# Grouped-query attention: the output projection in rounded parts, and its slots moved

## The chip, the cores and the metric

The kernel runs on one core of one Trainium2 chip. The metric is the device time of one execution in microseconds (us); the lower, the better. The page of the profile and the trace come from one profiled execution.

## What is computed

The program is eight layers on one stream x of 1024 tokens by 256, each of them `x = x + layer(layernorm(x))`: masked attention, a mixture of experts, a gated convolution, the mixture again, a selective scan, a second mixture, grouped-query attention, and the second mixture again. The change lies in the grouped-query attention alone. Cut to what matters:

```python
q = rms_norm(x @ Wq, q_norm_w)          # 32 heads of 128
k = rms_norm(x @ Wk, k_norm_w)          # 4 heads of 128
v = x @ Wv
q, k = rope(q), rope(k)
attn = softmax(causal(q @ k.T / sqrt(128)))
return (attn @ v) @ Wo                  # Wo: 4096 x 256
```

## The kernel before, in words

`gqa_layer` writes out the program of each engine by hand; engines meet only at semaphores. The 32 heads are 8 quads of four, which share one key head; 1024 tokens are 8 blocks of 128. One query tile is a quad's four heads for one block, so there are 64 tiles. Two tiles, a narrow one (block t) and a wide one (block 7 - t), make a **band** with 9 blocks of keys between them; t is 0, 1, 2, 3 in turn, so the wide tile has 1024, 896, 768 or 640 columns of scores. There are 32 bands, counted from 0, and each has 9 **slots**, 0 to 8. In slots 0 to 7 TensorE does one score job each (even slots the narrow tile, odd slots the wide one, one head a job), and in every slot it transposes and weighs one cell (one block of keys of the band before). Other work has its slot by a table: a tile's queries are projected in slots 0 and 6 (`query_tile`, "project"), transposed in slots 2 and 4 ("turn"), and the output projection of a tile, in two halves of two heads each, stands in slots 1, 3, 5 and 7 (`out_pair`).

Per slot and engine, in the order of the queue:

- TensorE: the score (L1333, its mask last, L1335), the transposes of a cell's probabilities (L1343), the query projection (L1268) or the transposes of queries (L1278), the output projection (L1366), and the weighing of the cell before (L1354).
- VectorE: the row maximum (L1226), the first add of the slot before's projection into the stream (L1219), the low part of the cell (L1231), the second add, then rope (L1149 to L1151) of the slot before's query projection or the low part of queries (L1156). Adds thus come one slot after their projection.
- ACT: the copy of a finished tile's output out of PSUM (L1106), the high part of the cell (L1112), the exponentials (L1121), the sums of squares of queries (L1056) or their high part (L1063).
- POOL: the scale of each query tile and the sum and product that end its rope (L1019 to L1027).

Queries are projected into, and transposed into, one PSUM bank (`q_bank`). So `turn_queries(n)` of slot 2 waits until the rope of the tile that slot 0 projected has read the bank, and `project(n)` until the queries before are read:

```python
pe.wait_ge(q_ready, n + 1)
if n % 2:
    pe.wait_ge(q_low_ready, n)
else:
    pe.wait_ge(roped, n + 2)
```

Most operands are split beforehand into a rounded high part and a low part (`F32R`), and `three` gives three matmuls of such parts for one product. The output projection is the exception: it multiplies `oT` and `wo` in plain fp32, two matmuls a half. The output weights of two quads lie in `wo` side by side, and query weights in `w_q` are replaced by SP once their split is done. In the profile's names `gqa_ln_xn` holds the queries after rope, `acc` and `aux` are PSUM, and `stream` is x.

Of the kernel before, what the change touches and what calls it, by code (L numbers as in the profile page):

```python
# [11 lines left out]
F32 = mybir.dt.float32  # L12
F32R = mybir.dt.float32r
# [3 lines left out]
ALU = mybir.AluOpType  # L17
# [3 lines left out]
P = 128  # L21
# [776 lines left out]
def gqa_layer(nc, core, wq_dram, wkv_dram, wo_dram, norm_w_dram, cos_dram, sin_dram):  # L798
# [5 lines left out]
    with ExitStack() as ctx:  # L804
# [4 lines left out]
        norm = Norm(nc, core, ctx, sem, "gqa", whole=False)  # L809
        RING = 4  # L810
        w_q = sb("w_q", [P, DC * QUAD * HD])
        w_q_high = sb("w_q_high", [P, DC * QUAD * HD], F32R)
        w_q_low = sb("w_q_low", [P, DC * QUAD * HD], F32R)
        wo = sb("wo", [P, 2, QUAD, D])
        norm_w = sb("norm_w", [P, 2, HD])
# [25 lines left out]
        sin_k = early[:, 8192:9216].rearrange("p (t d) -> p t d", d=HD)  # L841
        w_kv_high, w_kv_low = probsT_high, probsT_low
        straight = norm.xn[:, 0:4, :].rearrange("p (r a) d -> p r (a d)", r=2)
# [9 lines left out]
        w_q_in = sem("w_q_in")  # L853
        wo_in = [sem("wo_in0"), sem("wo_in1")]
        made = sem("made")
# [43 lines left out]
        TILES = 2 * BANDS  # L899
        SLOTS = CELLS * (BANDS + 1) + 5  # L900

# [37 lines left out]
        def out_pair(z):  # L939

            band, c = divmod(z, CELLS)
            n, half = {1: (2 * band - 3, 0), 3: (2 * band - 3, 1), 5: (2 * band - 2, 0), 7: (2 * band - 2, 1)}.get(c, (-1, 0))
            return (n, half) if 0 <= n < TILES else None
# [5 lines left out]
        def new_quad(z, at):  # L949

            band, c = divmod(z, CELLS)
            return band // 4 + 1 if c == at and band % 4 == 2 and band // 4 + 1 < QUADS else None

        block = ctx.enter_context(nc.Block())

        @block.sync
        def _(sp):
            def load_q(quad):
                sp.dma_start(w_q[:, :], wq_dram[quad:quad + 1].rearrange("a p k n -> (a p) (k n)")).then_inc(w_q_in, 16)

            def load_wo(quad):
                sp.dma_start(wo[:, quad % 2, :, :], wo_dram[quad:quad + 1].rearrange("a h p n -> p (a h) n")).then_inc(wo_in[quad % 2], 16)

            sp.dma_start(w_kv, wkv_dram.rearrange("g p k n -> p g (k n)")).then_inc(w_kv_in, 16)
            load_q(0)
            sp.dma_start(norm_w[:, :, :].rearrange("p a d -> p (a d)"),
                         norm_w_dram.rearrange("(b a) d -> b (a d)", b=1).to_broadcast([P, 2 * HD])).then_inc(norm_w_in, 16)
            sp.dma_start(core.xnT[:, 0, :], cos_dram.rearrange("p t d -> p (t d)")).then_inc(tables_in, 16)
            sp.dma_start(core.xnT[:, 1, :], sin_dram.rearrange("p t d -> p (t d)")).then_inc(tables_in, 16)
            load_wo(0)  # L970
            load_wo(1)
            for quad in range(1, QUADS):
                sp.wait_ge(w_q_low_ready, quad)
                load_q(quad)
                if quad >= 2:
                    sp.wait_ge(wo_done, 2 * NT * (quad - 1))
                    load_wo(quad)

        @block.gpsimd
        def _(pool):  # L980
# [54 lines left out]
            keys(3)  # L1035
            for n in range(3, TILES):
                queries(n)

        @block.scalar
        def _(act):  # L1040
            norm.scalar(act)

            def split_q(quad):
                act.wait_ge(w_q_in, 16 * quad + 16)
                if quad >= 1:
                    act.wait_ge(projected, NT * quad)
                act.activation(w_q_high[:, :], w_q[:, :], ACT.Copy).then_inc(w_q_high_ready, 1)

# [36 lines left out]
            for g in range(KV):  # L1085
                act.activation(w_kv_high[:, g, :], w_kv[:, g, :], ACT.Copy).then_inc(w_kv_high_ready, 1)
            split_q(0)
# [13 lines left out]
            for z in range(SLOTS):  # L1101
                for n in ended(z):
                    act.wait_ge(weighed, last_cell(n) + 1)
                    if n >= 2:
                        act.wait_ge(wo_done, 2 * (n - 1))
                    act.activation(oT[:, n % 2, :], out_bank, ACT.Copy).then_inc(oT_copied, 1)  # L1106
# [23 lines left out]
                if quad is not None:  # L1130
                    split_q(quad)

        @block.vector
        def _(dve):
            norm.vector(dve)

            def split_q(quad):
                dve.wait_ge(w_q_high_ready, quad + 1)
                dve.tensor_tensor(w_q_low[:, :], w_q[:, :], w_q_high[:, :].bitcast(F32), ALU.subtract).then_inc(w_q_low_ready, 1)

# [42 lines left out]
            for g in range(KV):  # L1183
                dve.wait_ge(w_kv_high_ready, g + 1)
                dve.tensor_tensor(w_kv_low[:, g, :], w_kv[:, g, :], w_kv_high[:, g, :].bitcast(F32), ALU.subtract).then_inc(w_kv_low_ready, 1)
            split_q(0)
# [35 lines left out]
            for z in range(SLOTS + 1):  # L1222
# [25 lines left out]
                if quad is not None:  # L1248
                    split_q(quad)

        @block.tensor
        def _(pe):
# [1210 lines left out]
```

## Time and profile before

| what | value |
|---|---|
| median of the runs shown | 1947.77 us (1946.73 to 1949.39, 3 runs) |
| the profiled execution | 1948.34 us |
| its span | 1946.4 us |
| busy: TensorE, VectorE, ACT, POOL | 80%, 65%, 48%, 34% of the span |
| granted TensorE clock, mean over the span | 0.888 |

The profiled execution is 1.9 us longer than its span and 0.6 us over the median. The grouped-query attention takes the span's part from some 930 us to 1800 us. The shares above are means over all layers; what a change in this layer is worth is read from this layer's stretch. PEclk is the TensorE clock that was granted, 1.00 for 2.4 GHz and 0.50 for 1.2 GHz. A matmul's shown end is modelled and overlaps the next one's start, so the time of one matmul in a row of them is read from start to start. In a timeline row the first number is the start in the span, the second the length, and the bracket the idle time of the engine ahead of it with what ended it.

### The profile page before, as it was taken

The page shows a single profiled execution, that of the slowest core. Times are in us where ns is not written, and L with a number is a line of the kernel's source. Part 1 is how long each engine was busy: PE and PEld are TensorE (multiplying, and loading weights), DVE is VectorE, ACT ScalarE, POOL GpSimd, SP SyncE. Part 2 cuts the span into 40 slices and gives each one's busy share as a digit, 9 for nine tenths or more (in the row PEclk, how much of TensorE's full clock was granted, in tenths as well). Part 3 has the DMA queues.
Part 4 walks back from the last instruction along what each step waited for, and adds up shares of the span by engine and source line. Part 5 has one row for each costly group of instructions (what it writes and reads, how often), then busy time and mean ns, then how long its engine had stood idle before and what let it go on. Part 6 is the DMA issues. An engine that isn't in the chain of part 4 may idle for free. (4 is left out here: it accounts for less than half of the span.)

```text
span 1946.4 us, 28135 instructions
## 1 busy us (share of the span) xinstructions
PE 1556.5 (80%) x9150; PEld 1214.7 (62%) x9158; DVE 1264.2 (65%) x2128; ACT 931.6 (48%) x2281; POOL 658.9 (34%) x671
## 2 busy tenths in 40 slices
PE   6899789779864565382769999999999999998373
PEld 4444578668851222272648888888888888886262
DVE  4665354665466998544737777777777777775533
ACT  2365344234424331252536666666666666664341
POOL 3011260415057674704832222222222222220703
PEclk9899799888987888586879999999999999999586
DMA  3321333213420000444000000000000000000443
GB/s 75 53 50 45 115 101 125 76 50 112 127 61 0 0 1 21 153 142 135 25 0 12 1 23 1 23 1 23 1 23 1 23 1 12 1 1 1 163 142 103
DMA packets 75322, 98.28 MB, mean 50 GB/s; under 512 B 11168, under 2 KB 58912, under 8 KB 75184
## 3 DMA queue, kind: packets, MB, share of 16 engines
q1 hardware_dynamic: 69040, 79.71, 13.9%
q0 software_dynamic: 6144, 16.79, 2.7%
q8 instruction: 79, 1.29, 0.3%
q14 instruction: 59, 0.48, 0.1%
HBM read 62.38 MB, written 27.66 MB: 46 GB/s over the span
## 5 line engine op out<-in xcount | busy, mean ns | idle before, releaser
L1226 DVE TENSOR_REDUCE gqa_neg_max<-acc 128x1 f32<-128x1024 f32 (+7 forms) x256 | 192.9, 754 | 175.6 <-PE acc L1335 174.4
L1112 ACT ACTIVATE gqa_probsT_high<-aux 128x512 fp32r<-128x512 f32 x288 | 172.0, 597 | 249.9 <-PE aux L1343 249.1
L1231 DVE TENSOR_TENSOR gqa_probsT_low<-aux,gqa_probsT_high 128x512 fp32r<-128x512 f32 x288 | 197.6, 686 | 29.8 <-ACT gqa_probsT_high L1112 25.5
L1121 ACT ACTIVATE gqa_probs<-acc,gqa_neg_max 128x1024 f32<-128x1024 f32 (+7 forms) x256 | 189.3, 740 | 29.8 <-DVE gqa_neg_max L1226 24.8
L1343 PE MATMUL aux<-ident,gqa_probs 128*128 128x128 f32 x1152 | 174.3, 274 | 0.0
L1354 PE MATMUL aux<-gqa_probsT_high,gqa_v_high 128*128 128x512 f32 x288 | 146.5, 509 | 1.0 <-DVE gqa_probsT_low L1231 1.0
L1019 POOL TENSOR_SCALAR gqa_q_scale<-gqa_q_scale 128x4 f32<-128x4 f32 x64 | 16.3, 255 | 383.4 <-ACT gqa_square L1056 383.1
L1366 PE MATMUL aux<-gqa_wo,gqa_oT 128*128 128x256 f32 x512 | 132.3, 381 | 4.4 <-DVE stream L1219 3.4
L1333 PE MATMUL acc<-gqa_k_low,gqa_q_high 128*128 128x512 f32 (+5 forms) x384 | 132.3, 345 | 0.0
L1333 PE MATMUL acc<-gqa_k_high,gqa_q_low 128*128 128x512 f32 (+5 forms) x384 | 132.0, 344 | 0.0
L1333 PE MATMUL acc<-gqa_k_high,gqa_q_high 128*128 128x512 f32 (+5 forms) x384 | 130.6, 340 | 1.6 <-DVE gqa_k_low L1181 1.6
L1023 POOL TENSOR_TENSOR gqa_ln_xn<-gqa_ln_xn 128x512 f32<-128x512 f32 x64 | 82.2, 1284 | 146.8 <-DVE gqa_ln_xn L1151 146.8
L1343 PEld LDWEIGHTS aux<-ident,gqa_probs 128*128 128x128 f32 x1152 | 124.5, 141 | 5.5
L1219 DVE SCALAR_TENSOR_TENSOR stream<-aux,gqa_row_inv,stream 128x256 f32<-128x256 f32 x256 | 121.2, 474 | 5.4 <-PE aux L1366 5.3
L2289 DVE TENSOR_TENSOR_SCAN scan_h<-scan_decay,scan_dbu 128x1024 f32<-128x1024 f32 x32 | 113.2, 3576 | 7.7 <-POOL scan_dbu L2213 7.0
L2213 POOL TENSOR_TENSOR scan_dbu<-scan_du,scan_b_all 128x1024 f32<-128x1024 f32 x32 | 106.3, 3343 | 33.9 <-ACT scan_b_all L2243 22.6
L458 POOL DMA_INDIRECT f_ln_xn<-outputs_by_slot,f_index x32 | 32.5, 1014 | 240.7 <-DMA outputs_by_slot<-f_y_tile 232.1
L1354 PE MATMUL aux<-gqa_probsT_low,gqa_v_high 128*128 128x512 f32 x288 | 113.9, 396 | 0.0
L1354 PE MATMUL aux<-gqa_probsT_high,gqa_v_low 128*128 128x512 f32 x288 | 113.3, 393 | 0.0
L622 DVE TENSOR_TENSOR f_part_low<-aux,f_part_high 128x384 fp32r<-128x384 f32 (+2 forms) x120 | 61.9, 517 | 69.5 <-ACT f_part_high L508 60.9
L700 PE MATMUL aux<-ident,f_xs 128*128 128x128 f32 x216 | 43.7, 288 | 74.8 <-issue 63.9
L1366 PEld LDWEIGHTS aux<-gqa_wo,gqa_oT 128*128 128x128 f32 x512 | 87.3, 190 | 12.7 <-issue 3.5
(397 smaller groups left out, 4452.4 us busy)
## 6 DMA issues: line engine op xcount, KB each, us to landing
f_w<-in_f_up SPq DMA_DIRECT2D x64, 256.0 KB, 2.7
f_xs<-tokens_by_slot SPq DMA_DIRECT2D x108, 128.0 KB, 2.1
outputs_by_slot<-f_y_tile SPq DMA_DIRECT2D x108, 128.0 KB, 1.7
f_w<-in_f_down SPq DMA_DIRECT2D x64, 128.0 KB, 3.0
mat_qk<-mat_high SPq DMA_DIRECT2D x64, 64.0 KB, 2.3
gqa_w_q<-in_g_wq SPq DMA_DIRECT2D x8, 512.0 KB, 3.6
gqa_wo<-in_g_wo SPq DMA_DIRECT2D x8, 512.0 KB, 3.8
tokens_by_slot<-zeros SPq DMA_DIRECT2D x1, 3968.0 KB, 13.2
```

The source lines that it names most:

```text
L1023: pool.tensor_tensor(straight[:, n % 2], straight[:, n % 2], swapped[:, n % 2], ALU.add).then_inc(q_summed, 1)
L1112: act.activation(probsT_high[:, u % RING, :], aux[:, u % 2, :], ACT.Copy).then_inc(cell_high_ready, 1)
L1121: act.activation(out, scores(n), ACT.Exp, bias=neg_max[:, j % (2 * JOBS):j % (2 * JOBS) + 1], accum_out=row_sum[:, n // 2 % 4, m, n % 2:n ...
L1219: dve.scalar_tensor_tensor(core.x[:, t, :], wo_bank[:, m * D:(m + 1) * D], row_inv[:, n // 2 % 4, 2 * half + m, n % 2:n % 2 + 1], core.x[: ...
L1226: dve.tensor_reduce(neg_max[:, j % (2 * JOBS):j % (2 * JOBS) + 1], scores(n), AXY, ALU.max, negate=True).then_inc(max_ready, 1)
L1231: dve.tensor_tensor(probsT_low[:, u % RING, :], aux[:, u % 2, :], probsT_high[:, u % RING, :].bitcast(F32), ALU.subtract).then_inc(cell_lo ...
L1333: pe.matmul(out[:, h, :], a, b, start=c == 0, stop=c == 2 and h < side)
L1343: last = pe.transpose(aux[:, u % 2, m * P:(m + 1) * P], head_probs(n, m)[:, s * P:(s + 1) * P], core.ident[:, :])
L1354: last = pe.matmul(out_bank, a, b, start=s + c == 0, stop=(s, c) == (tile_of(n), 2))
L1366: last = pe.matmul(wo_bank[:, m * D:(m + 1) * D], oT[:, n % 2, head * P:(head + 1) * P], wo[:, quad % 2, head, :], start=True, stop=True)
L2213: pool.tensor_tensor(dbu[:, 2 * (j % 2) + k], du[:, k], b_all[:, j % 4], ALU.mult).then_inc(dbu_ready, 1)
L2289: dve.tensor_tensor_scan(h[:, m], decay[:, m], dbu[:, m], 0.0, ALU.mult, ALU.add).then_inc(h_ready, 1)
```

## The change

The output projection now multiplies parts: ACT copies a finished tile's output to `oT` as before, POOL rounds it to `oT_high` and subtracts to `oT_low`, and each head's product is three matmuls instead of one in plain fp32. The output weights are split by ACT and VectorE in two halves per quad, at the ends of slots 4 and 6 of every fourth band (`wo_part`). The projections of a tile stand in slots 3, 5, 7 and the next band's slot 0, in place of 1, 3, 5 and 7. One raw buffer, `w_raw`, takes query weights and output weights in turn, `w_q` and the two-quad `wo` are gone, and the ring of the cells' parts has three buffers for four. The layer has one slot more at its end.

```diff
-        RING = 4
-        w_q = sb("w_q", [P, DC * QUAD * HD])
+        RING = 3
+        w_raw = sb("w_raw", [P, DC * QUAD * HD])
...
-        wo = sb("wo", [P, 2, QUAD, D])
+        wo_high = sb("wo_high", [P, QUAD, D], F32R)
+        wo_low = sb("wo_low", [P, QUAD, D], F32R)
...
+        oT_high = sb("oT_high", [P, 2, QUAD * P], F32R)
+        oT_low = sb("oT_low", [P, 2, QUAD * P], F32R)
...
+        wo = w_raw[:, :].rearrange("p (h n) -> p h n", h=QUAD)
...
-        SLOTS = CELLS * (BANDS + 1) + 5
+        SLOTS = CELLS * (BANDS + 1) + 6
...
-            n, half = {1: (2 * band - 3, 0), 3: (2 * band - 3, 1), 5: (2 * band - 2, 0), 7: (2 * band - 2, 1)}.get(c, (-1, 0))
+            n, half = {3: (2 * band - 3, 0), 5: (2 * band - 3, 1), 7: (2 * band - 2, 0), 0: (2 * band - 4, 1)}.get(c, (-1, 0))
...
+        def wo_part(z):
+
+            band, c = divmod(z, CELLS)
+            return (band // 4, {4: 0, 6: 1}[c]) if c in (4, 6) and band % 4 == 1 and band // 4 < QUADS else None
...
-            load_wo(0)
-            load_wo(1)
-            for quad in range(1, QUADS):
-                sp.wait_ge(w_q_low_ready, quad)
-                load_q(quad)
-                if quad >= 2:
-                    sp.wait_ge(wo_done, 2 * NT * (quad - 1))
-                    load_wo(quad)
+            for quad in range(QUADS):
+                if quad >= 1:
+                    sp.wait_ge(wo_low_ready, 2 * quad)
+                    load_q(quad)
+                sp.wait_ge(w_q_low_ready, quad + 1)
+                load_wo(quad)
...
-            for n in range(3, TILES):
-                queries(n)
+
+            def outputs(n):
+                pool.wait_ge(oT_copied, n + 1)
+                if n >= 2:
+                    pool.wait_ge(wo_done, 2 * (n - 1))
+                pool.tensor_copy(oT_high[:, n % 2, :], oT[:, n % 2, :]).then_inc(oT_high_ready, 1)
+                pool.wait_ge(oT_high_ready, n + 1)
+                pool.tensor_tensor(oT_low[:, n % 2, :], oT[:, n % 2, :], oT_high[:, n % 2, :].bitcast(F32),
+                                   ALU.subtract).then_inc(oT_low_ready, 1)
+
+            for z in range(SLOTS):
+                for n in ended(z):
+                    outputs(n)
+                n = query_tile(z - 1, "project")
+                if n is not None:
+                    queries(n)
...
-                        act.wait_ge(wo_done, 2 * (n - 1))
+                        act.wait_ge(oT_low_ready, n - 1)
...
+                if wo_part(z):
+                    quad, half = wo_part(z)
+                    act.wait_ge(wo_in, 16 * quad + 16)
+                    if quad >= 1:
+                        act.wait_ge(wo_done, 2 * NT * quad - 1 + half)
+                    act.activation(wo_high[:, 2 * half:2 * half + 2, :], wo[:, 2 * half:2 * half + 2, :], ACT.Copy).then_inc(wo_high_ready, 1)
...
+                if wo_part(z):
+                    quad, half = wo_part(z)
+                    dve.wait_ge(wo_high_ready, 2 * quad + half + 1)
+                    dve.tensor_tensor(wo_low[:, 2 * half:2 * half + 2, :], wo[:, 2 * half:2 * half + 2, :],
+                                      wo_high[:, 2 * half:2 * half + 2, :].bitcast(F32), ALU.subtract).then_inc(wo_low_ready, 1)
...
-                pe.wait_ge(oT_copied, n + 1)
-                if half == 0:
-                    pe.wait_ge(wo_in[quad % 2], 16 * (quad // 2) + 16)
+                pe.wait_ge(oT_low_ready, n + 1)
+                pe.wait_ge(wo_low_ready, 2 * quad + half + 1)
...
-                    last = pe.matmul(wo_bank[:, m * D:(m + 1) * D], oT[:, n % 2, head * P:(head + 1) * P], wo[:, quad % 2, head, :],
-                                     start=True, stop=True)
+                    rows = slice(head * P, (head + 1) * P)
+                    for c, (a, b) in enumerate(three(oT_high[:, n % 2, rows], oT_low[:, n % 2, rows], wo_high[:, head, :], wo_low[:, head, :])):
+                        last = pe.matmul(wo_bank[:, m * D:(m + 1) * D], a, b, start=c == 0, stop=c == 2)
```

How the change moves instructions, at three places. A row gives the line, the operation, what it writes and reads, the shape, and how many stand in a row.

VectorE, slots 1 and 2 of a band, before: the maximum, the low part and the rope of slot 1 (the three rows on `gqa_ln_xn`), then slot 2 with its two adds.

```order
L1226 TENSOR_REDUCE gqa_neg_max<-acc 128x1
L1231 TENSOR_TENSOR gqa_probsT_low<-aux,gqa_probsT_high 128x512
L1149 TENSOR_TENSOR gqa_ln_xn<-acc,xnT 128x512
L1150 TENSOR_TENSOR gqa_ln_xn<-acc,xnT 128x4x64
L1151 TENSOR_TENSOR gqa_ln_xn<-acc,xnT 128x4x64
L1226 TENSOR_REDUCE gqa_neg_max<-acc 128x1
L1219 SCALAR_TENSOR_TENSOR stream<-aux,gqa_row_inv,stream 128x256
L1231 TENSOR_TENSOR gqa_probsT_low<-aux,gqa_probsT_high 128x512
L1219 SCALAR_TENSOR_TENSOR stream<-aux,gqa_row_inv,stream 128x256
```

The same two slots now; the adds (L1251) stand in slot 1, round the low part and ahead of the rope, and slot 2 has none.

```order
L1258 TENSOR_REDUCE gqa_neg_max<-acc 128x1
L1251 SCALAR_TENSOR_TENSOR stream<-aux,gqa_row_inv,stream 128x256
L1263 TENSOR_TENSOR gqa_probsT_low<-aux,gqa_probsT_high 128x512
L1251 SCALAR_TENSOR_TENSOR stream<-aux,gqa_row_inv,stream 128x256
L1181 TENSOR_TENSOR gqa_ln_xn<-acc,xnT 128x512
L1182 TENSOR_TENSOR gqa_ln_xn<-acc,xnT 128x4x64
L1183 TENSOR_TENSOR gqa_ln_xn<-acc,xnT 128x4x64
L1258 TENSOR_REDUCE gqa_neg_max<-acc 128x1
L1263 TENSOR_TENSOR gqa_probsT_low<-aux,gqa_probsT_high 128x512
```

TensorE, before, from the mask that ends the score of slot 1 to the turned queries of slot 2 (a band whose narrow tile has 128 columns).

```order
L1335 MATMUL acc<-gqa_below,gqa_ident_b 128x128
L1343 MATMUL aux<-ident,gqa_probs 128x128 x4
L1366 MATMUL aux<-gqa_wo,gqa_oT 128x256 x2
L1354 MATMUL aux<-gqa_probsT_high,gqa_v_high 128x512
L1354 MATMUL aux<-gqa_probsT_low,gqa_v_high 128x512
L1354 MATMUL aux<-gqa_probsT_high,gqa_v_low 128x512
L1333 MATMUL acc<-gqa_k_high,gqa_q_high 128x128
L1333 MATMUL acc<-gqa_k_low,gqa_q_high 128x128
L1333 MATMUL acc<-gqa_k_high,gqa_q_low 128x128
L1335 MATMUL acc<-gqa_below,gqa_ident_b 128x128
L1343 MATMUL aux<-ident,gqa_probs 128x128 x4
L1278 MATMUL acc<-ident,gqa_ln_xn 128x128 x4
```

The same stretch now; the projection between the transposes and the weighing of slot 1 is gone.

```order
L1372 MATMUL acc<-gqa_below,gqa_ident_b 128x128
L1380 MATMUL aux<-ident,gqa_probs 128x128 x4
L1391 MATMUL aux<-gqa_probsT_high,gqa_v_high 128x512
L1391 MATMUL aux<-gqa_probsT_low,gqa_v_high 128x512
L1391 MATMUL aux<-gqa_probsT_high,gqa_v_low 128x512
L1370 MATMUL acc<-gqa_k_high,gqa_q_high 128x128
L1370 MATMUL acc<-gqa_k_low,gqa_q_high 128x128
L1370 MATMUL acc<-gqa_k_high,gqa_q_low 128x128
L1372 MATMUL acc<-gqa_below,gqa_ident_b 128x128
L1380 MATMUL aux<-ident,gqa_probs 128x128 x4
L1315 MATMUL acc<-ident,gqa_ln_xn 128x128 x4
```

TensorE, now, in slot 0 of the same band, from the query projection's last matmul to the first of the weighing.

```order
L1305 MATMUL acc<-gqa_w_q_high,xnT_low 128x512
L1404 MATMUL aux<-gqa_wo_high,gqa_oT_high 128x256
L1404 MATMUL aux<-gqa_wo_low,gqa_oT_high 128x256
L1404 MATMUL aux<-gqa_wo_high,gqa_oT_low 128x256
L1404 MATMUL aux<-gqa_wo_high,gqa_oT_high 128x256
L1404 MATMUL aux<-gqa_wo_low,gqa_oT_high 128x256
L1404 MATMUL aux<-gqa_wo_high,gqa_oT_low 128x256
L1391 MATMUL aux<-gqa_probsT_high,gqa_v_high 128x512
```

A projection of six matmuls stands there, where the weighing followed the query projection at once.

## Rows read from the trace of the kernel before

**Rows 1.** Windows view, 1500 to 1600 us: length, busy by engine, PEclk, DMA.
```profile
1500.00:1600.00 100.00, 98.92 (x579) 83.11 (x578) 76.63 (x140) 64.56 (x184) 28.73 (x32) 1.00 0.04 12
```

**Rows 2.** Waits of TensorE, 1060 to 1770 us: total, times, longest.
```profile
PE acc L1278 <- DVE gqa_ln_xn L1151: 6.6, 21, 0.5
```

**Rows 3.** TensorE's timeline (start, length), slots 1 and 2, 896 columns.
```profile
1511.27 0.23 PE L1335 MATMUL acc<-gqa_below,gqa_ident_b 128*128 128x128 bf16 x1
1511.78 1.03 PE L1366 MATMUL aux<-gqa_wo,gqa_oT 128*128 128x256 f32 x4
1514.70 0.63 PE L1278 MATMUL acc<-ident,gqa_ln_xn 128*128 128x128 f32 x4 [0.33 <-DVE gqa_ln_xn L1151]
```

**Rows 4.** The page's group of the output projection's matmuls (busy, mean ns | idle).
```profile
L1366 PE MATMUL aux<-gqa_wo,gqa_oT 128*128 128x256 f32 x512 | 132.3, 381 | 4.4 <-DVE stream L1219 3.4
```

**Rows 5.** Timeline: key and value projection, first and last of 28 matmuls.
```profile
949.79 0.28 PE L1291 MATMUL acc<-gqa_probsT_high,xnT_low 128*128 128x256 f32 x1
...
953.03 0.28 PE L1291 MATMUL aux<-gqa_probsT_high,xnT_low 128*128 128x256 f32 x1
```

**Rows 6.** Lines view by form: weight loads of rounded parts (busy, mean ns).
```profile
L1354 PEld LDWEIGHTS aux<-gqa_probsT_low,gqa_v_high 128*128 128x128 f32 x288 | 54.8, 190 | 5.8
```

**Rows 7.** VectorE's timeline: an add and its successor, then slot 1 of rows 3.
```profile
1507.15 0.47 DVE L1219 SCALAR_TENSOR_TENSOR stream<-aux,gqa_row_inv,stream 128x256 f32<-128x256 f32 x1
1507.54 0.68 DVE L1231 TENSOR_TENSOR gqa_probsT_low<-aux,gqa_probsT_high 128x512 fp32r<-128x512 f32 x1
...
1511.54 1.09 DVE L1226 TENSOR_REDUCE gqa_neg_max<-acc 128x1 f32<-128x896 f32 x1 [1.88 <-PE acc L1335]
1512.61 0.69 DVE L1231 TENSOR_TENSOR gqa_probsT_low<-aux,gqa_probsT_high 128x512 fp32r<-128x512 f32 x1
```

**Rows 8.** TensorE's timeline, slots 1 and 2 of band 1, without an output projection.
```profile
1014.60 0.23 PE L1335 MATMUL acc<-gqa_below,gqa_ident_b 128*128 128x128 bf16 x1
...
1018.04 0.63 PE L1278 MATMUL acc<-ident,gqa_ln_xn 128*128 128x128 f32 x4 [1.20 <-DVE gqa_ln_xn L1151]
```

**Rows 9.** Timeline, slots 1 and 2 of bands with 1024, 768 and 640 columns.
```profile
1489.55 0.63 PE L1278 MATMUL acc<-ident,gqa_ln_xn 128*128 128x128 f32 x4 [0.46 <-DVE gqa_ln_xn L1151]
...
1536.28 0.96 DVE L1226 TENSOR_REDUCE gqa_neg_max<-acc 128x1 f32<-128x768 f32 x1 [1.77 <-PE acc L1335]
1537.35 0.69 DVE L1231 TENSOR_TENSOR gqa_probsT_low<-aux,gqa_probsT_high 128x512 fp32r<-128x512 f32 x1
1539.45 0.63 PE L1278 MATMUL acc<-ident,gqa_ln_xn 128*128 128x128 f32 x4 [0.15 <-DVE gqa_ln_xn L1151]
...
1561.18 0.82 DVE L1226 TENSOR_REDUCE gqa_neg_max<-acc 128x1 f32<-128x640 f32 x1 [1.60 <-PE acc L1335]
1562.26 0.69 DVE L1231 TENSOR_TENSOR gqa_probsT_low<-aux,gqa_probsT_high 128x512 fp32r<-128x512 f32 x1 [0.25 <-ACT gqa_probsT_high L1112]
```

**Rows 10.** Lines view, POOL, 1060 to 1770 us.
```profile
L1023 POOL TENSOR_TENSOR gqa_ln_xn<-gqa_ln_xn 128x512 f32<-128x512 f32 x56 | 72.0, 1286 | 136.4 <-DVE gqa_ln_xn L1151 136.4
```

**Rows 11.** TensorE's timeline near the layer's start: three idles.
```profile
993.69 1.09 PE L1278 MATMUL acc<-ident,gqa_ln_xn 128*128 128x128 f32 x4 [2.26 <-DVE gqa_ln_xn L1151]
...
999.24 0.63 PE L1278 MATMUL acc<-ident,gqa_ln_xn 128*128 128x128 f32 x4 [1.60 <-DVE gqa_q_low L1156]
...
1010.36 0.66 PE L1268 MATMUL acc<-gqa_w_q_high,xnT_high 128*128 128x512 f32 x1 [1.75 <-DVE gqa_ln_xn L1151]
```

**Rows 12.** Windows view behind those three idles and behind that of rows 8.
```profile
993.70:997.00 3.30, 3.30 (x10) 2.54 (x11) 0.04 (x1) 1.05 (x3) 2.23 (x2) 0.53 0.00 0
1000.30:1003.60 3.30, 3.07 (x11) 2.07 (x9) 0.97 (x1) 0.27 (x1) 0.00 (x0) 0.50 0.00 0
1010.50:1013.80 3.30, 3.30 (x9) 2.64 (x10) 0.84 (x3) 1.25 (x8) 2.10 (x2) 0.50 0.00 0
1018.10:1022.00 3.90, 3.90 (x25) 3.31 (x25) 2.03 (x4) 1.83 (x5) 2.19 (x2) 1.00 0.02 4
```

**Rows 13.** The page's DMA issues (KB each, us to landing).
```profile
gqa_w_q<-in_g_wq SPq DMA_DIRECT2D x8, 512.0 KB, 3.6
```

More of the change, by code:

```diff
@@ L841, in gqa_layer @@
         sin_k = early[:, 8192:9216].rearrange("p (t d) -> p t d", d=HD)
-        w_kv_high, w_kv_low = probsT_high, probsT_low
+        w_kv_high = [probsT_high[:, 0, :], probsT_high[:, 1, :], probsT_high[:, 2, :], oT_high[:, 0, :]]
+        w_kv_low = [probsT_low[:, 0, :], probsT_low[:, 1, :], probsT_low[:, 2, :], oT_low[:, 0, :]]
+        wo = w_raw[:, :].rearrange("p (h n) -> p h n", h=QUAD)
         straight = norm.xn[:, 0:4, :].rearrange("p (r a) d -> p r (a d)", r=2)
@@ L853, in gqa_layer @@
         w_q_in = sem("w_q_in")
-        wo_in = [sem("wo_in0"), sem("wo_in1")]
+        wo_in = sem("wo_in")
+        wo_high_ready = sem("wo_high_ready")
+        wo_low_ready = sem("wo_low_ready")
         made = sem("made")
@@ L893, in gqa_layer @@
         oT_copied = sem("oT_copied")
+        oT_high_ready = sem("oT_high_ready")
+        oT_low_ready = sem("oT_low_ready")
         wo_done = sem("wo_done")
@@ L958, in load_q @@
             def load_q(quad):
-                sp.dma_start(w_q[:, :], wq_dram[quad:quad + 1].rearrange("a p k n -> (a p) (k n)")).then_inc(w_q_in, 16)
+                sp.dma_start(w_raw[:, :], wq_dram[quad:quad + 1].rearrange("a p k n -> (a p) (k n)")).then_inc(w_q_in, 16)
             def load_wo(quad):
-                sp.dma_start(wo[:, quad % 2, :, :], wo_dram[quad:quad + 1].rearrange("a h p n -> p (a h) n")).then_inc(wo_in[quad % 2], 16)
+                sp.dma_start(wo, wo_dram[quad:quad + 1].rearrange("a h p n -> p (a h) n")).then_inc(wo_in, 16)
             sp.dma_start(w_kv, wkv_dram.rearrange("g p k n -> p g (k n)")).then_inc(w_kv_in, 16)
@@ L1046, in split_q @@
                     act.wait_ge(projected, NT * quad)
-                act.activation(w_q_high[:, :], w_q[:, :], ACT.Copy).then_inc(w_q_high_ready, 1)
+                act.activation(w_q_high[:, :], w_raw[:, :], ACT.Copy).then_inc(w_q_high_ready, 1)
             def squares(n):
@@ L1085, in _ @@
             for g in range(KV):
-                act.activation(w_kv_high[:, g, :], w_kv[:, g, :], ACT.Copy).then_inc(w_kv_high_ready, 1)
+                act.activation(w_kv_high[g], w_kv[:, g, :], ACT.Copy).then_inc(w_kv_high_ready, 1)
             split_q(0)
@@ L1138, in split_q @@
                 dve.wait_ge(w_q_high_ready, quad + 1)
-                dve.tensor_tensor(w_q_low[:, :], w_q[:, :], w_q_high[:, :].bitcast(F32), ALU.subtract).then_inc(w_q_low_ready, 1)
+                dve.tensor_tensor(w_q_low[:, :], w_raw[:, :], w_q_high[:, :].bitcast(F32), ALU.subtract).then_inc(w_q_low_ready, 1)
             def rope(n):
@@ L1184, in _ @@
                 dve.wait_ge(w_kv_high_ready, g + 1)
-                dve.tensor_tensor(w_kv_low[:, g, :], w_kv[:, g, :], w_kv_high[:, g, :].bitcast(F32), ALU.subtract).then_inc(w_kv_low_ready, 1)
+                dve.tensor_tensor(w_kv_low[g], w_kv[:, g, :], w_kv_high[g].bitcast(F32), ALU.subtract).then_inc(w_kv_low_ready, 1)
             split_q(0)
@@ L1289, in kv @@
                         for m, (a, b) in enumerate(three(core.xnT_high[:, k, tokens], core.xnT_low[:, k, tokens],
-                                                         w_kv_high[:, g, cols], w_kv_low[:, g, cols])):
+                                                         w_kv_high[g][:, cols], w_kv_low[g][:, cols])):
                             last = pe.matmul(kv_banks[t // 2][:, t % 2 * 2 * HD:(t % 2 + 1) * 2 * HD], a, b,
```

## The prediction, made before the changed kernel ran

> **What bounds the kernel now.** I read the windows view first. In the steady part of this layer TensorE is busy 98.92 us of 100, at a granted clock of 1.00 (2.4 GHz); VectorE, next, 76.63 us [rows 1]. So work taken from TensorE shows in the time, and so does every wait put into its queue. The waits view names the only wait that it has there: the turned queries (L1278) wait for VectorE's rope (L1151), 21 times, 6.6 us in all [rows 2]. Then I read the timelines round that place. In slot 2 of each band TensorE transposes queries into the bank that the rope of slot 1 reads, so it must wait for that rope, and the rope stands last in VectorE's slot 1, behind the row maximum and the low part. In rows 3 the score of slot 1 ends with the mask at 1511.27 and the transposes start at 1514.70, 3.43 us later, after 0.33 us idle. Band 1 has no output projection in its slot 1; there the same stretch is 1018.04 - 1014.60 = 3.44 us [rows 8], and only the idle is longer (1.20 us). The reader is to see that VectorE's chain sets this stretch, whether or not TensorE has a projection to do meanwhile.
>
> **The projection itself.** Now a pair is two fp32 matmuls, four passes in the trace. They take 1.03 us with the last one's 0.38 in it [rows 3, 4], so passes start (1.03 - 0.38) / 3 = 0.217 us apart, and a pair is 0.87 us. Afterwards it is six rounded matmuls over 256 columns. The trace has such a series: 28 of them from 949.79 to 953.03, 0.12 us apart [rows 5]. Six make 0.72 us: 0.15 less a pair, 19 us over 128 pairs if that were all. The upper end is that loading weights (0.19 us [rows 6]) would not hide: 1.14 us, 0.27 more a pair. I take 0.72, since in rows 5 each matmul loads its own weights as well.
>
> **The move, 1, 3, 5, 7 to 3, 5, 7, 0.** Per band:
> - Slots 3, 5 and 7 keep a pair each: -3 x 0.15 = -0.45 us.
> - Slot 1 loses its pair. That gains nothing, since VectorE's chain sets the stretch [rows 3, 8]; TensorE only idles 0.87 us more.
> - Slot 0 gets a pair where TensorE has no idle time: +0.72 us.
> - The two adds of that pair now stand in VectorE's slot 1, one ahead of the low part and one behind it, and both ahead of the rope. An add holds up its successor by 1507.54 - 1507.15 = 0.39 us [rows 7], two by 0.78. With 1024 and 896 columns the low part follows the maximum at once (1.09 us long, next start 1.07 later [rows 7]), so all of it counts. With 768 and 640 columns the low part already starts 1.07 and 1.08 us after a maximum of 0.96 and 0.82 [rows 9], because ACT is later; the first add fits into 0.11 and 0.26 of that. The rope comes 0.78, 0.78, 0.67 and 0.52 us later.
>
> The wait exists in bands 2 to 30 (band 31 has no queries left to turn, band 1 no pair in slot 0): 29 bands, 7 each with 1024, 896 and 640 columns and 8 with 768. Sum: 29 x (0.72 - 0.45) = 7.8, and 7 x (0.78 + 0.78 + 0.52) + 8 x 0.67 = 19.9: **+27.7 us**.
>
> **What lies beside.** POOL gets a copy and a subtraction per tile. Its addition over the same 512 columns takes 1.29 us [rows 10]; I take that for the subtraction and as the upper end of the copy, 2.6 us at most. A band is 1514.70 - 1489.55 = 25.15 us [rows 3, 9], a slot some 2.8. The parts are wanted two slots after ACT's copy, so they are early; and the queries queued behind them on POOL wait for a rope that comes later still, and are wanted in slot 4. If POOL took two slots, slot 7's pair would wait instead. ACT's 16 splits of the output weights and VectorE's 16 stand at the ends of slots 4 and 6 in one band of four, ahead of a score that VectorE waits for anyway; uncovered they would cost at most 16 x 0.69 = 11 us by the low part of rows 7, and I take 0. SP now loads the query weights only after those splits, at slot 6, three slots or 8 us ahead of their use; landing takes 3.6 us [rows 13]. Without that cover ACT would stand still, seven times. RING 3 for 4 costs nothing, since the weighing that frees the third buffer stands two slots earlier in TensorE's queue. The 12 pairs outside bands 2 to 30 save 12 x 0.15 = 1.8 us, and the last tile of the layer waits for POOL with nothing beside it, 2.6 at most: I take +1. With the clock as it is, the execution's 1948.3 becomes **1977 us**. The shown runs' median, 1947.8, lies 0.6 below that execution; I leave that out.
>
> **The clock.** The idle ahead of the turned queries grows by 0.87 plus the shift: from 0.46, 0.33 and 0.15 us [rows 3, 9] to 2.11, 1.98 and 1.69, and with 640 columns to about 1.39. Near the layer's start TensorE had idles of 2.26, 1.60 and 1.75 us [rows 11], and behind each the granted clock stood near 0.5, which is 1.2 GHz, for the 3.3 us shown [rows 12]; behind an idle of 1.20 it stayed at 1.00 [rows 8, 12]. So in 22 of the 29 bands the new idle has the size of those that were followed by a fall. Such a stretch does 3.3 us of work at half speed, 1.65 us lost, and TensorE has no slack behind it. Three cases don't show that every idle of that size does it: the ends are none, and all 29 (48 us). I take 14 of the 22, nearer to what three of three say: **+23 us**, 2000 us. The Trainium skill (TensorE: Matmul & The Clock Gate, Why this matters for your kernels) warns of throughput drops mid-kernel only for idle gaps longer than any of these; by that rule the term would be 0 and the sum 1977. The trace differs, since 1.60 us was enough [rows 11, 12].
>
> **Rivals.**
> - *The idle without the clock* (0.24): the waits come as worked out, but the granted clock stays at 1.00, so 1977 us. For it: behind 1.20 us it stayed [rows 8, 12], and the steady part runs at 1.00 [rows 1]. Against it: the three falls. This is what the skill's rule just named would give.
> - *TensorE's saving shows* (0.08), the other sign: slot 0's pair merely replaces slot 1's, the rope isn't later than TensorE, and 128 x 0.15 = 19 us come off: 1929 us. It decides at the transposes of slot 2: the rope would have to end 0.87 us sooner after the mask than now. Against it: rows 8, where TensorE came early and still waited.
> - *Weight loads show* (0.05): a pair costs 1.14 us, 0.42 more than taken, in four slots of 29 bands: +49, so 2049 us with the clock's share. Against it: rows 5.
> - *The move does less than it says* (0.05): part of the new idle is taken back by a wait later in the band that I don't see now, and the time ends between 1940 and 1965.
>
> **How the numbers follow.** My forecast, idle with a clock that falls in about half of the bands, has 0.58, and its own range is 1985 to 2024 (5 to 29 bands). The predicted time is 2000 us. The range of 8 in 10 must take in the rival of 1977 with some doubt in the shift (0.3 us a band, 9 us): 1968 to 2024. It leaves out the saving, the weight loads and most of the last rival. No change means within 0.2%, about 4 us, which is what a measurement of this kernel can tell. Faster: 0.08 and a little of the last rival, 0.09; same 0.02; slower 0.89.
>
> **What would show it.** In the changed profile: rounded projection matmuls 0.12 us apart; TensorE idle ahead of the turned queries in slot 2, some 1.4 to 2.1 us, released by the rope, 45 to 55 us in the waits view; both adds ahead of the rope on VectorE; no wait of TensorE for POOL's parts or the output weights; granted clock below 1.00 in the layer's windows, behind slot 2. I am wrong if that idle stays below 1 us, or if the projection waits for POOL, or if the granted clock falls nowhere.

## The result, and the profile after

The changed kernel takes 1990.55 us (median of 4 runs, 1988.96 to 1996.81) against 1947.94 us of the kernel before on the same chip. The ratio is 1.0223, with a 95% interval from 1.0208 to 1.0239: slower by 42.6 us. The forecast was 2000 us, in a range from 1968 to 2024. The profiled execution of the change took 1988.96 us, with a span of 1986.1; its four runs differ as their mean granted clock does (0.885, 0.880, 0.885, 0.883 for 1988.96, 1996.81, 1990.39, 1990.71 us). The difference between the two spans is 1986.1 - 1946.4 = 39.7 us.

First the windows view of the change, the steady stretch of rows 1.

```profile
1500.00:1600.00 100.00, 93.07 (x565) 78.59 (x564) 71.87 (x131) 61.11 (x169) 43.10 (x46) 0.97 0.04 12
```

TensorE was busy 98.92 us of 100 [rows 1] and is now busy 93.07, and the granted clock is no longer 1.00 throughout. The waits of TensorE, 1060 to 1820 us, say what it waits for:

```profile
PE acc L1315 <- DVE gqa_ln_xn L1183: 48.4, 28, 2.1
PE aux L1404 <- DVE stream L1251: 0.8, 1, 0.8
```

It is the wait of rows 2, grown from 6.6 to 48.4 us. No row names the new parts on POOL or the output weights. TensorE's timeline shows slots 1 and 2 of the band with 896 columns that follows the one at 1091 us (columns: start, length). The first row is the mask of slot 1, the third that of slot 2.

```profile
1113.36 0.23 PE L1372 MATMUL acc<-gqa_below,gqa_ident_b 128*128 128x128 bf16 x1
1113.43 0.61 PE L1380 MATMUL aux<-ident,gqa_probs 128*128 128x128 f32 x4
...
1114.92 0.23 PE L1372 MATMUL acc<-gqa_below,gqa_ident_b 128*128 128x128 bf16 x1
1114.99 0.61 PE L1380 MATMUL aux<-ident,gqa_probs 128*128 128x128 f32 x4
1117.50 0.63 PE L1315 MATMUL acc<-ident,gqa_ln_xn 128*128 128x128 f32 x4 [1.91 <-DVE gqa_ln_xn L1183]
```

From the mask of slot 1 to the turned queries it is 1117.50 - 1113.36 = 4.14 us, where rows 3 have 3.43: 0.71 more, although TensorE has a projection less to do there. VectorE's timeline of the same slot 1 shows why.

```profile
1113.63 1.09 DVE L1258 TENSOR_REDUCE gqa_neg_max<-acc 128x1 f32<-128x896 f32 x1 [2.45 <-PE acc L1372]
1114.64 0.47 DVE L1251 SCALAR_TENSOR_TENSOR stream<-aux,gqa_row_inv,stream 128x256 f32<-128x256 f32 x1
1115.03 0.68 DVE L1263 TENSOR_TENSOR gqa_probsT_low<-aux,gqa_probsT_high 128x512 fp32r<-128x512 f32 x1
1115.63 0.47 DVE L1251 SCALAR_TENSOR_TENSOR stream<-aux,gqa_row_inv,stream 128x256 f32<-128x256 f32 x1
1116.02 0.68 DVE L1181 TENSOR_TENSOR gqa_ln_xn<-acc,xnT 128x512 f32<-128x512 f32 x1
1116.62 0.41 DVE L1182 TENSOR_TENSOR gqa_ln_xn<-acc,xnT 128x256 f32<-128x256 f32 x1
1116.95 0.41 DVE L1183 TENSOR_TENSOR gqa_ln_xn<-acc,xnT 128x256 f32<-128x256 f32 x1
```

From the maximum to the end of the rope VectorE has no idle time, and both adds (0.39 us each until the next starts) lie inside, ahead of the rope. The turned queries start 0.14 us after it ends. What happens behind such a wait is shown by two groups of three consecutive bands (1024, 896 and 768 columns each). TensorE's timeline, the turned queries of slot 2:

```profile
1194.30 0.63 PE L1315 MATMUL acc<-ident,gqa_ln_xn 128*128 128x128 f32 x4 [2.10 <-DVE gqa_ln_xn L1183]
1220.71 0.63 PE L1315 MATMUL acc<-ident,gqa_ln_xn 128*128 128x128 f32 x4 [1.91 <-DVE gqa_ln_xn L1183]
1246.62 0.63 PE L1315 MATMUL acc<-ident,gqa_ln_xn 128*128 128x128 f32 x4 [1.61 <-DVE gqa_ln_xn L1183]
...
1297.49 0.63 PE L1315 MATMUL acc<-ident,gqa_ln_xn 128*128 128x128 f32 x4 [2.10 <-DVE gqa_ln_xn L1183]
1325.45 0.91 PE L1315 MATMUL acc<-ident,gqa_ln_xn 128*128 128x128 f32 x4 [1.91 <-DVE gqa_ln_xn L1183]
1352.94 0.63 PE L1315 MATMUL acc<-ident,gqa_ln_xn 128*128 128x128 f32 x4 [1.60 <-DVE gqa_ln_xn L1183]
```

Windows view behind the waits at 1194.30 and 1297.49 (columns as in rows 1):

```profile
1194.40:1198.00 3.60, 3.60 (x24) 3.03 (x25) 1.43 (x2) 1.48 (x4) 2.15 (x2) 1.00 0.02 5
1298.40:1301.60 3.20, 3.20 (x9) 2.09 (x8) 0.00 (x0) 0.36 (x1) 1.35 (x2) 0.50 0.00 0
```

Both follow an idle of 2.10 us. Behind the first the granted clock stays at 1.00 (2.4 GHz), and the band takes 1220.71 - 1194.30 = 26.41 us; behind the second it is 0.50 (1.2 GHz) and the band takes 1325.45 - 1297.49 = 27.96, 1.55 more. For the bands behind them, with a fall in the second group again, it is 1246.62 - 1220.71 = 25.91 and 1352.94 - 1325.45 = 27.49, 1.58 more. Such a fall costs some 1.56 us. The trace has 8 of them in the steady part (bands 2 to 30), behind 8 of the 14 idles of 1.91 and 2.10 us and behind none of the shorter ones, 1.60 and 1.29 us.

**Where the 39.7 us are.** Four bands without a fall take 1194.30 - 1091.09 = 103.21 us, and the four at that place took 1191.46 - 1092.08 = 99.38 before: 0.96 us a band, 27.8 over 29. The 8 falls make 8 x 1.56 = 12.5. The first turned queries of band 1 start 3.56 us sooner than before (1014.48 against the 1018.04 of rows 8; 2.02 of it stands already at 991.67 against the 993.69 of rows 11, and one fall fewer behind that makes the rest), and the layer's end and the stages behind it account for what is left, 39.7 - 27.8 - 12.5 + 3.6 = 3.0 us.

### The profile page after: what moved, and what is told of

The parts are those of the page before. It is cut to its first block and busy times, and to the rows that moved or that the text cites. A ratio compares the mean times of both kernels' runs of the same rounds, so it can differ in the third digit from the quotient of the medians.

```text
span 1986.1 us, 28884 instructions
## 1 busy us (share of the span) xinstructions
PE 1549.0 (78%) x9406; PEld 1215.0 (61%) x9414; DVE 1268.9 (64%) x2144; ACT 941.3 (47%) x2297; POOL 785.9 (40%) x799
## 5 line engine op out<-in xcount | busy, mean ns | idle before, releaser
L1391 PE MATMUL aux<-gqa_probsT_high,gqa_v_high 128*128 128x512 f32 x288 | 126.8, 440 | 0.3 <-ACT gqa_oT L1132 0.3
L1251 DVE SCALAR_TENSOR_TENSOR stream<-aux,gqa_row_inv,stream 128x256 f32<-128x256 f32 x256 | 121.6, 475 | 7.4 <-PE aux L1404 7.3
L1053 POOL CAST gqa_oT_high<-gqa_oT 128x512 fp32r<-128x512 f32 x64 | 39.1, 610 | 158.9 <-ACT gqa_oT L1132 158.9
L508 ACT ACTIVATE f_part_high<-aux 128x384 fp32r<-128x384 f32 (+2 forms) x120 | 55.7, 464 | 69.7 <-PE aux L700 66.4
```

The costliest lines, as they stand in the source:

```text
L1251: dve.scalar_tensor_tensor(core.x[:, t, :], wo_bank[:, m * D:(m + 1) * D], row_inv[:, n // 2 % 4, 2 * half + m, n % 2:n % 2 + 1], core.x[: ...
L1391: last = pe.matmul(out_bank, a, b, start=s + c == 0, stop=(s, c) == (tile_of(n), 2))
```

## The experiments

The theory was: VectorE's rope ends late because two adds stand ahead of it; slot 1's missing projection gives nothing back; and the clock falls behind part of the new idles. The rivals: POOL or the rounded projection itself holds TensorE up, or the clock's part is something else. All ratios are to the kernel before, with 95% intervals. Differences in us are to the medians above, 1947.94 and 1990.55; beside the experiments the kernel before took 1947.44 to 1948.03 us.

**The projection back in slot 1, rounded parts kept.** The tables of projections, with slot 0's pair put into slot 1 of the same band:

```diff
-            n, half = {3: (2 * band - 3, 0), 5: (2 * band - 3, 1), 7: (2 * band - 2, 0), 0: (2 * band - 4, 1)}.get(c, (-1, 0))
+            n, half = {1: (2 * band - 4, 1), 3: (2 * band - 3, 0), 5: (2 * band - 3, 1), 7: (2 * band - 2, 0)}.get(c, (-1, 0))
```

> The changed kernel with the fourth projection in slot 1 instead of slot 0 (the same tile's second half, one slot later); all else as changed. Theory (the loss is the place of that pair: in slot 0 its two adds stand ahead of the rope, and slot 1 loses its cover): TensorE's idle ahead of the turned queries falls back to 0.15 us above that of the kernel before (0.6, 0.5, 0.3 and 0.15 us), the granted clock stays at 1.00, and each of 29 bands is 3 x 0.15 = 0.45 us shorter than before: about 13 us faster than before, 1935 us, with 3 us of doubt for the layer's end. Rival (the parts themselves cost the time: POOL's two operations, the splits of the output weights, three matmuls for one): the place changes little and the time stays above 1975 us.

Measured: 1937.76 us, ratio 0.9936 (0.9915 to 0.9956). Its waits of TensorE, 1060 to 1700 us:

```profile
PE acc L1315 <- DVE gqa_ln_xn L1183: 9.1, 19, 0.6
```

One table entry takes away 52.8 us. The longest idle is 0.60 us, and the granted clock falls nowhere in the steady part. So the loss is in the place of that pair, not in the parts.

**The rope ahead of the adds.** VectorE's slot 1, the pair staying in slot 0:

```diff
-                add(z - 1, 0)
+                late = z % CELLS == 1
+                if not late:
+                    add(z - 1, 0)
...
                         rope(n)
+                    if late:
+                        add(z - 1, 0)
+                        add(z - 1, 1)
```

(The second add is left out at its old place in the same way.)

> The changed kernel, except that in VectorE's slot 1 both adds come behind the rope. Theory: the rope is no longer late by 0.52 to 0.78 us, so TensorE's idle in slot 2 falls to 1.3, 1.2, 0.9 and 0.8 us (the lost cover stays), the granted clock stays at 1.00 in the steady part, and of the loss 20 us of shift and 12 us of clock go: about 1958 us, 0.5% above before. Rival (the cover alone makes the idle, the adds are hidden): 1980 us or more. Rival (adds that come later hold up the projection of slot 3, which waits for them): a new wait of TensorE at the projection, and over 1970 us.

Measured: 1961.72 us, ratio 1.0068 (1.0045 to 1.009). Waits of TensorE, 1060 to 1700 us:

```profile
PE acc L1321 <- DVE gqa_ln_xn L1183: 28.6, 26, 1.3
PE acc L1321 <- DVE gqa_q_low L1188: 1.8, 6, 0.3
```

The idles shrink from 2.10, 1.91, 1.60 and 1.29 us to 1.32, 1.20, 1.03 and 0.86, by 0.78, 0.71, 0.57 and 0.43: the adds' share, near the forecast shift of 0.78, 0.78, 0.67 and 0.52. The remaining idle is slot 1's lost cover: from mask to mask, in four bands, slot 1 is 0.86 or 0.87 us shorter than in the kernel before and slot 2 0.86 to 0.88 us longer, so what the pair took in slot 1 comes back whole as waiting. Behind idles of 1.32 and less no fall is left.

**The move alone, on the kernel before.** fp32 projections, in the slots of the change:

```diff
-        SLOTS = CELLS * (BANDS + 1) + 5
+        SLOTS = CELLS * (BANDS + 1) + 6
...
-            n, half = {1: (2 * band - 3, 0), 3: (2 * band - 3, 1), 5: (2 * band - 2, 0), 7: (2 * band - 2, 1)}.get(c, (-1, 0))
+            n, half = {3: (2 * band - 3, 0), 5: (2 * band - 3, 1), 7: (2 * band - 2, 0), 0: (2 * band - 4, 1)}.get(c, (-1, 0))
```

> The kernel before (projection in plain fp32, no parts), with its projections moved to slots 3, 5, 7 and 0. Theory: the move is the whole loss and the parts take a little of it back: idle in slot 2 as in the changed kernel (2.1, 1.9, 1.6, 1.3 us), each pair 0.87 us instead of 0.72, so 29 x (0.87 + 0.69) = 45 us and some 8 falls of the clock at 1.6 us: about 2005 us, 14 us above the changed kernel. Rival (POOL's and the weights' splits carry part of the loss): below the changed kernel's 1990 us.

Measured: 1997.69 us, ratio 1.0248 (1.0228 to 1.0269). Waits of TensorE, 1060 to 1700 us:

```profile
PE acc L1278 <- DVE gqa_ln_xn L1151: 41.5, 24, 2.1
```

The same idles come with the move alone, so neither POOL nor the parts make them. This execution had 4 falls in the steady part and not 8, worth 4 x 1.56 = 6.2 us, most of what it lies below the expected time.

**The idle filled.** Ahead of the turned queries of slot 2, TensorE multiplies zeros and adds the products, which are zero, to the bank of the weighing:

```diff
+            def fill(band):
+                if band % 4 == 1:
+                    pe.wait_ge(oT_copied, 2 * band - 1)
+                for _ in range(7 if band % 4 < 2 else 5):
+                    pe.matmul(out_bank, core.zeros[:, 0:P], core.zeros[:, :], start=False, stop=False, skip_group_check=True)
...
+                    if z % CELLS == 2 and z >= 2 * CELLS:
+                        fill(z // CELLS)
                     turn_queries(n)
```

> The changed kernel with matmuls of zeros (7 or 5 of 512 columns, bf16, added into the weighing's sum) ahead of the turned queries of slot 2, in bands 2 and on; they fill most of the wait and no result depends on it. Theory (of the loss about 12 us are stretches at 1.2 GHz behind the idle): the turned queries start as late as in the changed kernel, the recorded idle falls below 1 us, the granted clock stays at 1.00 from band 2 on, and the time falls by 8 to 13 us to about 1978 us although TensorE does more. Rival (the clock falls for another reason, or its falls cost nothing since VectorE is as late anyway): no change, 1988 to 1993 us, or longer by the filled matmuls.

Measured: 1978.76 us, ratio 1.015 (1.0128 to 1.0171). Windows view, the stretch of rows 1:

```profile
1500.00:1600.00 100.00, 97.85 (x607) 80.87 (x606) 73.03 (x132) 63.43 (x179) 43.41 (x47) 1.00 0.04 12
```

The bands still take 25.90 us (25.80 in the change without falls), so the rope is as late as in the change, but the clock stays at 1.00 and 11.8 us are gone. The 0.10 us more per band stand in one band of four, where the fill itself waits for ACT's copy; over 29 bands they are 2.9 us. So the clock's share is 11.8 + 2.9 = 14.7 us between the medians, near the 12.5 counted above in an execution that was 1.6 us shorter than its kernel's median. The rest of the loss, 1978.76 - 1947.94 = 30.8 us, is there without a fall: the 27.8 us by which the bands are longer, and the fill's 2.9.

**The parts in the old slots.** The change with the table of the kernel before, the weights' splits moved to slots 3 and 4 so that they come in time:

```diff
-            n, half = {3: (2 * band - 3, 0), 5: (2 * band - 3, 1), 7: (2 * band - 2, 0), 0: (2 * band - 4, 1)}.get(c, (-1, 0))
+            n, half = {1: (2 * band - 3, 0), 3: (2 * band - 3, 1), 5: (2 * band - 2, 0), 7: (2 * band - 2, 1)}.get(c, (-1, 0))
...
-            return (band // 4, {4: 0, 6: 1}[c]) if c in (4, 6) and band % 4 == 1 and band // 4 < QUADS else None
+            return (band // 4, {3: 0, 4: 1}[c]) if c in (3, 4) and band % 4 == 1 and band // 4 < QUADS else None
```

> The changed kernel with its projections in the slots of the kernel before, 1, 3, 5 and 7 (and the splits of the output weights in slots 3 and 4, to be in time). Theory (the parts need two slots between ACT's copy and the projection, which the old table does not give the wide tile): in slot 1 the projection waits 1.3 to 1.6 us for POOL's copy and subtraction, in every fourth band slot 5 too; no adds ahead of the rope. About +1 us a band, 1965 to 1985 us, with TensorE's waits named on the projection and not on the turned queries. Rival (POOL is quick enough, the old slots would do): 1935 to 1945 us, as with the fourth pair in slot 1.

Measured: 1996.06 us, ratio 1.0256 (1.0236 to 1.0276), slower than expected. Waits of TensorE, 1060 to 1700 us:

```profile
PE aux L1404 <- POOL gqa_oT_low L1055: 41.9, 31, 1.8
PE acc L1305 <- DVE gqa_q_low L1188: 3.8, 6, 0.6
```

The chain behind one of these waits, on ACT, POOL and TensorE (a timeline each):

```profile
1111.99 0.62 ACT L1132 ACTIVATE gqa_oT<-aux 128x512 f32<-128x512 f32 x1
```

```profile
1112.68 0.61 POOL L1053 CAST gqa_oT_high<-gqa_oT 128x512 fp32r<-128x512 f32 x1 [1.41 <-ACT gqa_oT L1132]
1113.37 1.27 POOL L1055 TENSOR_TENSOR gqa_oT_low<-gqa_oT,gqa_oT_high 128x512 fp32r<-128x512 f32 x1
```

```profile
1114.69 0.39 PE L1404 MATMUL aux<-gqa_wo_high,gqa_oT_high 128*128 128x256 f32 x1 [1.35 <-POOL gqa_oT_low L1055]
```

POOL's two operations end 2.03 us after ACT's copy (1114.64 - 1112.61), and TensorE waits for them. So the parts do need about a slot more than the old table gives them, which the change's later slots provide. The mechanism was the expected one; its size was not: these idles too were followed by a lower clock, 7 times, all behind idles of 1.78 or 1.79 us, which I had not counted. At 1.56 us each they are 10.9 of the 11.1 us above the forecast's end.

**Slot 1, and the rope first.** The table entry of the first experiment, and in VectorE's slot 1 the rope ahead of the low part:

```diff
                 add(z - 1, 0)
+                early = z % CELLS == 1 and query_tile(z - 1, "project") is not None
+                if early:
+                    rope(query_tile(z - 1, "project"))
...
-                    if n is not None:
+                    if n is not None and not early:
                         rope(n)
```

> The run with the fourth pair in slot 1, and the rope ahead of the low part in VectorE's slot 1. Theory (what is left of the idle, 0.60, 0.49, 0.32 and 0.14 us, is the rope standing behind the low part of 0.6 us): the turned queries no longer wait, a shorter wait for that low part may appear at the weighing of slot 2, and the time falls by 2 to 10 us to 1928 to 1936 us. Rival (the low part is as urgent as the rope): the wait only changes its name, 1936 to 1940 us.

Measured: 1923.18 us, ratio 0.9869 (0.9853 to 0.9886), the fastest kernel here: 24.8 us under the kernel before, 67.4 under the change. From 1060 to 1700 us the waits view names no wait of TensorE. Windows view, the stretch of rows 1:

```profile
1500.00:1600.00 100.00, 99.87 (x630) 84.98 (x630) 79.08 (x146) 67.89 (x190) 45.55 (x49) 1.00 0.04 12
```

The gain over the run with the fourth pair in slot 1 is 14.6 us, more than the 2 to 10 that were forecast. From mask to mask, in four bands, slot 2 is 1.85 us shorter and one slot 4 is 0.31 longer: some 11 us over 29 bands. Another 3.0 us stand ahead of the turned queries of band 1 (1014.53 against 1017.50), where this execution had one fall fewer.

**POOL's subtraction twice.** The change, with the subtraction of the low part done again over its own result; nothing is left out:

```diff
+                                   ALU.subtract).then_inc(oT_once, 1)
+                pool.wait_ge(oT_once, n + 1)
+                pool.tensor_tensor(oT_low[:, n % 2, :], oT[:, n % 2, :], oT_high[:, n % 2, :].bitcast(F32),
                                    ALU.subtract).then_inc(oT_low_ready, 1)
```

> The changed kernel with POOL's subtraction done twice for each tile, 64 x 1.3 us more on POOL ahead of the queries' scale. Theory (POOL's parts are early and the queries behind them wait for the rope, so POOL is off the path): no change but for the last tile of the layer, 1988 to 1999 us with the clock's falls by chance. Rival (POOL's queue sets when the turned queries of slots 2 and 4 come): TensorE waits for POOL's product of the rope, and some 0.5 to 1.3 us a band are added, 2005 us or more.

Measured: 1998.13 us, ratio 1.0253 (1.0233 to 1.0272). Waits of TensorE, 1060 to 1700 us:

```profile
PE acc L1319 <- DVE gqa_ln_xn L1187: 41.4, 24, 2.1
```

The idles are those of the change (2.10, 1.91, 1.60 and 1.29 us), and no wait for POOL appears, though POOL is busy for 50.36 us of 100 and not 43.10. The profiled span is 12.4 us longer than the change's; it has 12 falls in the steady part where the change has 8, and one more ahead of it: 5 x 1.56 = 7.8 us. Another 3.5 us stand ahead of the place of the first row of rows 11 (995.18 against 991.67), and the 1.1 left are about the last tile's wait for one more subtraction (4.0 us for 2.7). Why this execution had more falls is not shown; POOL being off the path is.

**The rope first, on the kernel before.** The edit on VectorE alone, with fp32 projections:

```diff
+                early = z % CELLS == 1 and query_tile(z - 1, "project") is not None
+                if early:
+                    rope(query_tile(z - 1, "project"))
...
-                    if n is not None:
+                    if n is not None and not early:
                         rope(n)
```

> The kernel before (fp32 projection, slots 1, 3, 5, 7), with the rope ahead of the low part in VectorE's slot 1, and nothing else changed. It measures the parts by themselves, against the run with the fourth pair in slot 1 and the same rope: both without a wait in slot 2. Theory (a pair in parts is 0.15 us shorter and nothing else of the change costs time then): 128 x 0.15 = 19 us, less 2 for the layer's last tile, above that run's 1923 us, so 1940 us; the idle in slot 2 of the kernel before, 8 us in the trace, goes. Rival (the rope's place made all of that run's gain, and the parts bring nothing): 1923 to 1928 us.

Measured: 1933.96 us, ratio 0.994 (0.9927 to 0.9954), between the two forecasts. So the order on VectorE gives 14.0 us, and the parts on top of it 1933.96 - 1923.18 = 10.8 us, not the 19 that 128 pairs at 0.15 us would give. The turned queries of slot 4 in a band with 768 columns show one place where the rest goes. TensorE's timeline of the kernel with fp32 projections, then VectorE's:

```profile
1531.79 0.61 PE L1346 MATMUL aux<-ident,gqa_probs 128*128 128x128 f32 x4
1532.23 0.60 PE L1281 MATMUL acc<-ident,gqa_ln_xn 128*128 128x128 f32 x4
```

```profile
1531.35 0.68 DVE L1156 TENSOR_TENSOR gqa_q_low<-acc,gqa_q_high 128x512 fp32r<-128x512 f32 x1
```

And the same place with the parts and slot 1 (the kernel of 1923.18 us):

```profile
1524.81 0.60 PE L1383 MATMUL aux<-ident,gqa_probs 128*128 128x128 f32 x4
1525.53 0.63 PE L1318 MATMUL acc<-ident,gqa_ln_xn 128*128 128x128 f32 x4
```

```profile
1524.71 0.68 DVE L1188 TENSOR_TENSOR gqa_q_low<-acc,gqa_q_high 128x512 fp32r<-128x512 f32 x1
```

With fp32 the transposes take 0.44 us until the turned queries start, 0.20 after VectorE's low part of the queries ended. With the parts TensorE arrives sooner, the low part ends at 1525.39, and the turned queries start 0.14 us later, 0.72 after the transposes: 0.28 us of waiting that the trace does not mark as idle, because the modelled end of the transposes (0.60) covers it. From mask to mask every slot with a projection is 0.13 to 0.17 us shorter in four such bands (one slot 7: 0.07), 2.33 us in all; six of the slots 2, 4 and 6 are 0.12 to 0.31 longer, 1.11 in all (the slot 4 above is the longest; what the other five wait for is not shown). What remains, with 0.02 in the other slots, is 1.24 us per four bands; it makes 9.0 of the 10.8 us over 29 bands.

## Why the prediction was right, and where it was off

- **What bounds.** Right: TensorE and, at one place, VectorE's chain from slot 1's mask to the rope. The move alone and the return to slot 1 show that the place of one pair decides some 50 us.
- **The projection, 0.15 us a pair.** The six matmuls are 0.12 us apart, as rows 5 said; the timeline of the change:

```profile
1099.66 0.28 PE L1404 MATMUL aux<-gqa_wo_low,gqa_oT_high 128*128 128x256 f32 x1
1099.78 0.28 PE L1404 MATMUL aux<-gqa_wo_high,gqa_oT_low 128*128 128x256 f32 x1
1099.90 0.28 PE L1404 MATMUL aux<-gqa_wo_high,gqa_oT_high 128*128 128x256 f32 x1
```

  So the rival in which weight loads show is out. But a pair's saving is no saving of time wherever VectorE's chain ends last a slot later; in the fastest kernel nearly half of it is given back.
- **The move, +27.7 us.** Right: 0.96 us a band by the trace, 27.8 in all. Of this the slot 1 row ("gains nothing") and the shift of the rope were tested one by one (in the run with the rope ahead of the adds), and the forecast idles of 2.11, 1.98, 1.69 and 1.39 us were 2.10, 1.91, 1.60 and 1.29. That the idles are a little shorter and the sum still fits is luck. From mask to mask, in the four bands from 1091 us, the shift is 2.50 us where the forecast has 2.75; slots 3, 5 and 7 save 1.73 and not 1.80, and slots 4 and 6, which the forecast left out, are 0.19 us longer in all.
- **What lies beside.** Right for POOL (twice the subtraction changes no idle), for the splits and for the single raw buffer: no wait of TensorE for any of them up to 1820 us. Behind that, at the layer's last tile, it waits for POOL once, 2.7 us, where the prediction had 2.6 at most. Two of POOL's rows in the change, lines view, 1060 to 1820 us:

```profile
L1055 POOL TENSOR_TENSOR gqa_oT_low<-gqa_oT,gqa_oT_high 128x512 fp32r<-128x512 f32 x59 | 76.1, 1290 | 4.8
...
L1053 POOL CAST gqa_oT_high<-gqa_oT 128x512 fp32r<-128x512 f32 x60 | 36.6, 610 | 148.2 <-ACT gqa_oT L1132 148.2
```

  The subtraction takes the 1.29 us of rows 10, the copy 0.61: 1.9 us, under the bound of 2.6. Their cover is the later slots; with the old slots the kernel takes 1996.06 us, no less than the change.
- **The clock, +23 us.** The mechanism was right, and this is the term that was mis-sized. Of "14 of the 22" idles at 1.65 us, the profiled execution shows 8, at 1.56: 12.5 us, and 14.7 by the filled idle, less than the 23 of the sum. The step that failed is that idles of 1.69 us would be as likely to be followed by a fall as those near 2.0: none of the 15 idles of 1.60 and 1.29 us in the steady part was, though 1.60 near the layer's start was [rows 11, 12]. The three cases in rows 11 stood among other idle times; those in the steady part stand some 25 us apart; whether that is what differs was not tried. In the old slots 7 of the 8 idles of 1.78 or 1.79 us were followed by a fall. How many falls an execution has does not follow from its idles: 4, 8 and 12 at the same ones. And "three of three" was partly luck: of the nine traces with the idle of 1.75 us near the layer's start, four show a fall behind it. The rival without the clock, 1977 us, is what the kernel with the filled idle came to, 1978.76. The Trainium skill (TensorE: Matmul & The Clock Gate, Why this matters for your kernels) speaks of mid-kernel drops only behind longer gaps; the 8 falls here stand behind idles of 1.91 and 2.10 us.
- **The rival of the other sign** (TensorE's saving shows) is out for this change: the turned queries started 0.71 us later after the mask, and not 0.87 sooner. It holds in part once the rope stands first and slot 1 has its pair again: 10.8 us, not 19.

Of the forecasts for the experiments, three missed their range or value by much: the parts in the old slots by the falls of the clock behind idles that I had costed at their length, the rope on the kernel before because the saving of the parts was taken whole, and slot 1 with the rope first, which gained some 11 us in the bands, 1 more than forecast, and 3.0 ahead of them. Two were forecast as one value: the rope ahead of the adds took 3.7 us more than that, the move alone 7.3 us less.

## What to carry to other kernels

Work on the busiest engine that stands beside another engine's chain is free, and moving it to a place without such cover costs its whole length; count the chain, not the busy share. Before an operation is moved, see what is queued behind its consumer: two adds of 0.39 us each, ahead of a value that the busiest engine waits for, cost more here (some 18 us, 2.50 per four bands) than the faster matmuls brought (10.8). Put first, in an in-order queue, what the bounding engine waits for: that edit alone brought 14 us.

## What the runs showed of the hardware that was not expected

- The clock's fall is not set by the length of the idle ahead of it alone. Idles of 1.91 and 2.10 us were followed by 1.2 GHz 8 times of 14 in the change, 12 times in the run with POOL's subtraction twice and 4 times with the move alone, at the same idles; runs of one kernel differ by up to 7.9 us, along with their mean granted clock.
- A wait of up to 0.28 us on TensorE can stand unmarked, under the modelled end of the matmuls ahead. The waits of rows 2 add up to 6.6 us, and the kernel before became 14.0 us faster when the rope was put first.
- Making the high part by a copy on POOL took 0.61 us, less than half of a subtraction over the same 512 columns (1.29 us).
